# Second attention of a two-layer block: scores by row bands instead of repeated queries and keys, probabilities as the stationary operand

## The reference, cut to what matters

```
x = x + tanh(g_xattn[0]) * attention0(layernorm(x), ctx)      # one head, stage A
x = x + tanh(g_ffn[0])   * experts0(layernorm(x))             # 16 experts of 64, top 4, one shared, stage B
x = x + tanh(g_xattn[1]) * attention1(layernorm(x), ctx)      # 16 heads of 8, stage C
x = x + tanh(g_ffn[1])   * experts1(layernorm(x))             # 8 experts of 128, top 2, stage D

# attention1, for each batch and each of the 16 heads
q = (x @ Wq.T + bq) / sqrt(8);  k = ctx @ Wk.T + bk;  v = ctx @ Wv.T + bv
p = softmax(q @ k.T)            # 128 x 77 for each head
out = concat(p @ v) @ Wo.T + bo
```

## Time and profile before

| | |
|---|---|
| Median of 3 runs | 331.32 us (330.4 to 331.4) |
| The profiled execution's own time | 328.63 us |
| Its span in the trace | 326.7 us, mean granted TensorE clock 0.979 |
| PE, weight loads, DVE, ACT, POOL busy | 289.0, 216.5, 243.6, 163.1, 103.4 us |
| Stages by the trace | A 0 to 39, B 39 to 135.7, C 135.7 to about 244, D to 326.7 us |

### The profile page before, as it was taken

How to read it: one execution, slowest core, us unless ns; L and a number is a source line. 1 busy time by engine, 2 the same in 40 slices (tenths; PEclk the granted TensorE clock), 3 DMA queues, 4 the chain that set the end, 5 groups by cost and what they waited for, 6 DMA issues and landing times.

```text
span 326.7 us, 5592 instructions
## 1 busy us (share of the span) xinstructions
PE 289.0 (88%) x1470; PEld 216.5 (66%) x1470; DVE 243.6 (75%) x714; ACT 163.1 (50%) x435; POOL 103.4 (32%) x160
## 2 busy tenths in 40 slices
PE   6699699989899599589888888988978999999995
PEld 5588476666566376268778778778856667676662
DVE  2887989689579976546697787877968877868572
ACT  1587542432422232676887887889742242332321
POOL 6374200101191510564549539629110010100000
PEclk9999999999979899959999999999999999999999
DMA  6900175586791420000000000000032242151550
GB/s 220 325 25 0 48 225 156 159 231 192 220 246 48 140 98 32 0 2 0 0 4 0 2 1 0 0 0 3 0 108 99 55 155 104 52 178 33 182 174 32
DMA packets 16408, 28.98 MB, mean 89 GB/s; under 512 B 2661, under 2 KB 4659, under 8 KB 16179
## 3 DMA queue, kind: packets, MB, share of 16 engines
q1 hardware_dynamic: 14312, 27.71, 27.6%
q10 hardware_dynamic: 2072, 0.99, 1.2%
HBM read 24.29 MB, written 1.25 MB: 78 GB/s over the span
## 4 chain that ended last, share of the span: by engine, by line
PE 59%; DVE 15%; ACT 9%; DMA 7%; issue 6%; SPq 4%; DVEq 1%; ACTq 0%
PE bank L564 23%; PE Ybank L586 14%; PE bank L757 4%; DMA CR<-comb_rows 3%; ACT PX L1025 3%; DVE cmx L1410 2%; DMA comb_rows<-ct 2%; PE Tb L503 2%; SPq L326 2%; DMA X<-in_x 2%; DVE recT L1426 2%; ACT QS L1013 1%; PE bank L741 1%; PE bank L602 1%; DVE st L1117 1%
## 5 line engine op out<-in xcount | busy, mean ns | idle before, releaser
L908 ACT ACTIVATE sg<-bank 128x512 f32<-128x512 f32 x64 | 38.0, 595 | 73.7 <-PE bank L564 62.0
L1277 DVE TENSOR_TENSOR hb<-sg,CR 128x512 f32<-128x512 f32 x64 | 44.6, 696 | 17.0 <-issue 7.0
L355 POOL TENSOR_TENSOR rstd<-ve,mhalf 128x4 f32<-128x4 f32 x11 | 11.1, 1011 | 131.5 <-DVE ve L1124 131.5
L1270 DVE TENSOR_TENSOR sg<-sg,bank 128x512 f32<-128x512 f32 x64 | 43.5, 680 | 4.5 <-ACT sg L908 2.2
L1410 DVE TENSOR_REDUCE cmx<-bank 128x4 f32<-128x308 f32 x64 | 28.3, 471 | 17.4 <-PE bank L730 17.2
L564 PE MATMUL bank<-xh,WBH 128*128 128x512 f32 x68 | 35.6, 524 | 5.4 <-DVE sg L1270 4.0
L372 POOL TENSOR_TENSOR KS<-kr,CB 128x1232 fp32r<-128x1232 f32 x16 | 36.2, 2268 | 11.3 <-PE bank L730 11.3
L564 PE MATMUL bank<-xh,UPH 128*128 128x512 f32 x64 | 36.2, 565 | 0.0
L586 PE MATMUL Ybank<-hb,W2T 128*128 128x512 f32 x64 | 33.8, 610 | 1.6 <-DVE hb L1277 1.6
L586 PE MATMUL Ybank<-hb,downw 128*128 128x512 f32 x64 | 32.9, 598 | 0.1
L1025 ACT ACTIVATE PX<-bank,cmx 128x77 f32<-128x77 f32 x128 | 29.3, 354 | 0.0
(11 more groups left out here) (184 smaller groups left out, 598.5 us busy)
## 6 DMA issues: line engine op xcount, KB each, us to landing
CR<-comb_rows SPq DMA_DIRECT2D x64, 128.0 KB, 3.2
CR<-comb_rows SPq DMA_DIRECT2D x32, 256.0 KB, 3.4
VX<-in_vs_seed SPq DMA_DIRECT2D x4, 320.0 KB, 5.5
kr<-kh SPq DMA_DIRECT2D x8, 154.0 KB, 3.2
kr<-kl SPq DMA_DIRECT2D x8, 154.0 KB, 3.3
w13raw<-in_w SPq DMA_DIRECT2D x1, 1088.0 KB, 11.4
X<-in_x SPq DMA_DIRECT2D x4, 256.0 KB, 6.5
upraw<-in_up SPq DMA_DIRECT2D x4, 256.0 KB, 4.5
```

The costliest lines, as they stand in the source:

```text
L355: nc.gpsimd.tensor_tensor(rstd[:], ve[:], mhalf[:], ALU.pow).then_inc(rstd_rdy, 1)
L908: A(sg[:, k % 2, :], Gb[k % 2][:], ACT.Silu).then_inc(m.s_done, 1)
L1270: V.tensor_tensor(sg[:, k % 2, :], sg[:, k % 2, :], Ub[k % 2][:], ALU.mult).then_inc(m.t2, 1)
L1277: V.tensor_tensor(hb[:, k % 2, :], sg[:, k % 2, :], CR[:, k % RING, :], ALU.mult).then_inc(m.h_done, 1)
```

## The change

The scores of four heads are made in one band of 32 rows: queries and keys stay where the projections leave them (head h in rows 8h to 8h+7), and each of the four bands has its own bank of PSUM. High and low parts are no longer stacked in rows, but are four matmuls that add up in the bank, so a batch has 16 score matmuls of 32 rows and 308 columns. `QS`, `kr`, `RQ`, `c_repeat` and `place_keys` go away, and POOL expands 616 columns for a batch in place of 1232. The maxima and subtractions take two banks at a time (616 columns), all exponentials have 616 columns and no bias. In the mix the transposed probabilities are stationary and `VX` moves: 9 columns for a head, 8 values and a one, so that the sum of a head comes out beside its result; the rest of the 128 columns are zeros that POOL writes once. The result has queries as rows, needs a reciprocal of 16 columns only, and is transposed (`c_turn`) before the projection; this turn and the projection's result lie in `Tb`. `upraw` lies on the memory of `w13raw` and is loaded first in `later_load`; the `vs_seed` input is gone. The `Fori` loops of stage C on PE, ACT and DVE become Python loops, that is straight code; POOL's stays.

```diff
 def later_load(n):
     if n == 0:
-        sp.wait_ge(k_l, NG)
-    if n < 8:
-        place_keys(2 * n)
-        place_keys(2 * n + 1)
-    elif n < 12:
+        sp.wait_ge(w_split, 10)
+    if n < 4:
...
         sp.dma_start(upraw[:, part], up[:, part]).then_inc(in_up, 16)
-    elif n < 14:
+    elif n < 6:
...
         sp.dma_start(downw[:, part, :], down[:, part, :]).then_inc(in_up, 16)
-    elif n < 18:
...
-        sp.dma_start(VX[:, (n - 14) // 2 * NC * P:((n - 14) // 2 + 1) * NC * P][:, half],
-                     vs_seed[:, half]).then_inc(in_seed, 16)
...
-nc.gpsimd.memset(RQ[:].bitcast(F32), 0.0).then_inc(built, 1)
+nc.gpsimd.memset(Vn[:, :, :, HD:HV], 1.0)
+nc.gpsimd.memset(qq[:, 0].bitcast(F32), 0.0).then_inc(built, 1)
...
 inv_std(NG + 2)
+nc.gpsimd.memset(VX[:], 0.0)
...
-def c_scores(g, t, s, first=False):
+def c_scores(g, t):
     n = GB * g + t
...
+    pe.wait_ge(ks_done, n + 1)
+    if n:
+        pe.wait_ge(c_sub, START + NU * n)
+    for a, b in ((0, 0), (0, 1), (1, 0), (1, 1)):
+        for s in range(NHG):
+            rows = slice(32 * s, 32 * (s + 1))
+            i = mm(bank[s][:, 0:HG * S], qq[rows, g % 2, a, t * P:(t + 1) * P], KT[rows, t % 2, b, :],
+                   start=a + b == 0, stop=a + b == 2)
+    i.then_inc(c_sc, 1)
...
-def c_mix(g, t, u, first):
+def c_mix(g, t, first):
...
+    for c in range(NC):
         w = chunk_rows(c)
-        i = mm(bOut[t % 2][:, u * P:(u + 1) * P], VX[0:w, v:v + P], pt[0:w, c * P:(c + 1) * P],
+        i = mm(bO9[c // CU], pt[0:w, t % 2, c * P:(c + 1) * P], VX[0:w, t % 2, c, :],
                start=c % CU == 0, stop=c % CU == CU - 1)
...
+def c_turn(g, t):
+    n = GB * g + t
+    pe.wait_ge(c_norm, START + n + 1)
+    pe.wait_ge(c_fin, START + n)
+    tr(bOT, On[:].rearrange("p h d -> p (h d)"), I).then_inc(c_ot, 1)
```

More of the change, by code:

```diff
@@ new lines, in c_body @@
+                    n = GB * g + t
+                    before = (g, t - 1) if t else None if first else (g - 1, GB - 1)
+                    if t < GB - 1:
+                        c_scores(g, t + 1)
+                    elif not last:
+                        c_scores(g + 1, 0)
+                    c_transpose(g, t, 0)
+                    if t == 1:
+                        pe.wait_ge(xl_rdy, NG + g + 2)
+                    if t == 2 and not last:
+                        pe.wait_ge(q_l, g + 2)
@@ L1015, in _ @@
[L1015 to L1030 removed]
+                A(qq[:, g % 2, 0, :], Tb[:], ACT.Identity, bias=cols[:, 1:2]).then_inc(q_h, 1)
@@ L1051, in c_body @@
                     n1 = (g, t + 1) if t + 1 < GB else (g + 1, 0)
+                    ahead = t + 1 < GB or not last
+                    c_copy(g, t, 0, first)
                     if t or not first:
[L1053 to L1057 removed]
+                        c_turned(*((g, t - 1) if t else (g - 1, GB - 1)))
+                    if t == GB - 1 and last:
+                        m_route_tanh(mD, 0)
+                    c_copy(g, t, 1, first)
+                    if ahead:
+                        c_exps(*n1, 0)
+                    c_copy(g, t, 2, first)
+                    if t == 0 and not first:
+                        norm_hi(2 * NG + 2 + g, xh[:, slot(g + 1):slot(g + 1) + GT])
                     if t == 1 and not last:
@@ L1060, in c_body @@
                     if t == GB - 1 and last:
-                        m_route_tanh(mD, 0)
                         m_route_copy(mD, 0)
-                    for s in range(NHG):
-                        if t + 1 < GB or not last:
-                            c_exps(*n1, s)
-                        if t == 2 and not last and s != 1:
-                            c_repeat(g + 1, (0, None, 1, 2)[s])
-                    if t == 0:
-                        norm_hi(2 * NG + 2 + g, xh[:, bass.ds(slot(g + 1), GT)])
+                    if ahead:
+                        c_exps(*n1, 1)
+                    if t == 0 and first:
+                        norm_hi(2 * NG + 2 + g, xh[:, slot(g + 1):slot(g + 1) + GT])
             def c_ahead(k):
@@ L1447, in c_body @@
                     before = (g, t - 1) if t else None if first else (g - 1, GB - 1)
-                    before2 = (g, t - 2) if t > 1 else None if first else (g - 1, t + 2)
                     ahead = t + 1 < GB or not last
-                    end = t == GB - 1 and last
+                    if before:
+                        c_normalize(*before)
                     if ahead:
                         c_max(*n1, 0)
-                    if before2:
-                        c_final(*before2)
+                        c_center(*n1, 0)
+                    else:
+                        route_weights(mD, 0)
@@ L1496, in _ @@
-            c_center(0, 0, 3, first=True)
             c_body(0, True, False)
-            with dve.Fori(1, NG - 1) as g:
+            for g in range(1, NG - 1):
                 c_body(g, False, False)
```

407 lines of the change are left out of this document (141 added, 266 removed).

## The result

The changed kernel takes 322.13 us (median of 4 runs, 319.98 to 324.81) against 331.36 us for the kernel before on the same chip (330.4 to 335.08): ratio 0.973, 95% interval 0.967 to 0.979. Ratios and their intervals leave out the runs that lie more than 1.5% above the fastest one of the same kernel; the medians count every run. The profiled execution took 322.10 us with a span of 320.3, 6.4 less than the span before. DVE is relieved a little (237.1 us busy in place of 243.6) and ACT much (129.9 in place of 163.1).

The account below looks back on a forecast made before the run. PE made up 59% of the chain, with PE, ACT and DVE nearly full in C. Terms summed to -8.3 us: 320.3 us profiled, 323.0 us median; range 316 to 329 for the likeliest mechanism, 315 to 339 for all.

Parts of the forecast that it names:

- Bands beside each other, S = 1.0: PE's 16 score matmuls per batch: four bands side by side, four rounds of load and streaming, 1.0 us; best case 0.56.
- rival of loads in a row: Scores of every batch: 16 weight loads pass one way into the array, 1.78 us; 336.1 us in all; chance 0.20.
- that of one after another: Scores of every batch: the 16 matmuls run singly, 2.24 us; 343.8 us in all; chance 0.08.
- The drain: Rival: each change between 32 and 128 rows costs 0.25 us with nothing issued; 331.4 us, no change; chance 0.14.
- T + 2.95: In a turn of C, the mix starts 2.95 us after the batch's first transposes, right behind ACT's third copy.
- Turns 1 to 15, -0.6: Stage C: 14 x 5.2 + 13 x 1.0 = 85.8 us against 86.4, a gain of 0.6.
- Hidden in that idle or behind it: Turns of C: result's turn, projection, norm's transposes, next queries (0.7 us) and DVE's second maximum, subtraction, statistics add no time.
- ACT's and DVE's relief gives room, not time: Stage C: work removed lies off the turn's path; sign: DVE and ACT each busy 4 to 5 us less in four turns.
- Begin, +0.3, at most +1.2: POOL zeroes VX while DVE normalises: 0.3 us lost, at most 1.2, as DVE waits for the ring in any case.
- Fourth and third group, -2.6 and -2.4: Stage B starts: halved key expansions shorten PE's wait, 2.6 us gained; downw loads gone from the ring's way, 2.4 gained.
- First turn, 0: First turn of C, 9.0 us with transposes at 1.2 GHz: PE idles there after the change too, no gain.
- Into C, out of C, end of B: Seams of stages: +1.4 us into C, -2.6 out of C, -1.4 at the end of B.

Follow-up runs that it names:

- copy-first run: Changed kernel with ACT's third copy ahead of the exponential and PE's projection behind the last transposes: 322.62 us, ratio 0.977 to the kernel before.
- early memset: Changed kernel with POOL zeroing VX ahead of its wait for the second group's statistics: 320.65 us, ratio 0.969 to the kernel before.
- bands in series: Changed kernel with the four score matmuls of one band following each other, then the next band: 325.27 us, ratio 0.982 to the kernel before.
- second run of the early memset: Changed kernel with VX zeroed before POOL's wait for statistics, repeated beside the joined versions: 321.0 us, ratio 0.967 to the kernel before.

## Why the prediction held, point by point

The median came at 322.1 us where 323.0 was forecast. That they agree within a us is in part luck: the difference of the profiled executions was -6.4 in place of -8.3, that of the medians -9.2, and several terms were off by 1.5 to 2.1 us in both directions and partly cancelled. The mechanism that was forecast for the scores, the bands beside each other, is the one that ran.

- **Bands beside each other, S = 1.0.** S was 0.77, nearer to the best case. Each band was given 0.11 for a load and 0.14 for streaming in every round; the later bunches of matmuls stand 0.14 us apart, so the loads are hidden after the first. The rival of loads in a row (1.78) and that of one after another (2.24) are refuted by the same 0.77, whatever the order. The drain is real, 0.17 us ahead of the scores and at most 0.13 behind, and too small to decide. One reading behind the loads was off: the 296 ns of the earlier trace rows are a mean of loads from 187 to 338 ns, and loads at half clock took 0.33 us in the kernel after; the 0.111 us of the router's pairs, on which the term rests as well, are not touched by it.
- **The mix as before, 2.26.** It took 2.40 to the first score matmul, 0.17 of it that drain. T + 2.95 was met within 0.01.
- **Turns 1 to 15, -0.6.** It came out +0.9. Thirteen plain turns of 6.13 and the last of 5.27 make 85.0; the other 2.3 us are the turns with the norm's transposes and the next queries (7.03 once, 6.29 to 6.54 otherwise). "Hidden in that idle or behind it" is the step that failed: PE's idle piece of 0.75 us stands ahead of the mix, and it is where these instructions and DVE's waits for them come in.
- **ACT's and DVE's relief gives room, not time.** Shown by the middle of C: ACT 8.5 us less in four turns, the turns 0.5 us shorter. The sign named for it, 4 to 5 us less for each engine, failed for both, ACT's relief being twice that and DVE's only 1.5 us. DVE lost the large reciprocal, but it now subtracts the maximum for all four portions, where ACT's bias did it for two: subtractions take 25.6 us in place of 15.2. That ACT's order sets the turn was argued from the path, and the copy-first run shows it (-0.56 us a turn).
- **Begin, +0.3, at most +1.2.** It cost 2.4, the mis-sized term of the sum. I let DVE's later wait for the ring (1.01 us) cover the memset. But PE doesn't wait for the products behind the ring: it waits for the key instruction that stands right behind the normalising, with no cover, and goes on at 1.2 GHz. Where the clock stayed up behind the same wait the cost was 1.1 us, inside the bound; the half clock, which the term left out, makes the rest. The early memset took back all of it. The Trainium skill ("SBUF — State Buffer", section "SBUF: two separate sides") calls the port pair of DVE and GpSimd an exclusive lock held for the whole instruction; the 2.52 us beside a memset of 2.23 agree, and show that a memset is enough.
- **Fourth and third group, -2.6 and -2.4.** -3.3 and -1.8. The normalising of the fourth group fell from 5.00 to 2.94 us with half of POOL's columns, as forecast; that the expansions cost this much there is shown by the kernel before with them moved, 4.8 us less in that group. At the third group the wait for the ring went as forecast, but POOL's `split_up` now meets the normalising (2.65): a wait that took the place of the one removed, which the sum had not. With that work early the third and fourth group took 1.1 and 1.8 us less again.
- **First turn, 0.** -1.8. It took 7.2 us here, and 6.5 to 9.6 in the profiles of the other versions; PE waits 3.36 to 3.41 us for DVE's subtraction ahead of it in all of them, and the half clock behind lasts longer or shorter; in the 6.5 there is none. That part of the gain is not the change's to claim.
- **Into C, out of C, end of B.** Within 0.4 us each.

What stays open: why the half clock behind the same wait of 3.37 us lasts for different lengths, or stays away, in one kernel, and stage D's +0.5 us, for which no run was made; D takes 79.0 to 79.3 us in the profiles of the changed kernel and its versions.

## What to carry to other kernels

Cut the contraction into row bands when operands would else have to be repeated: here 16 matmuls of 32 rows cost little more than four of 128, and the two orders tried cost the same within 0.03 us. Then look for what the freed engine leaves behind: the turn was set by the order of three copies and two exponentials on ACT, and swapping two of them, with the norm one batch earlier, was worth 4.7 us in turns that the change itself had not shortened. And price every instruction of POOL, a memset too, by which instruction of DVE it will meet and what PE waits for behind that.

## What the runs showed of the hardware that I had not expected

- DVE was held by POOL in large and small instructions that work on SBUF: four normalising instructions of 1.25 us together took 2.52 beside a memset, and four of 1.11 took 2.94 beside expansions of 2.61; a product of 0.69 took 2.76, a 16-column copy 2.21. But not in all: a reciprocal of 128x128 from SBUF to SBUF kept its 0.94 us beside an expansion, and in stage C DVE's maxima and subtractions that read PSUM kept their 0.80.
- Sixteen weight loads of 32 rows fit in 0.58 us, in an order that changes the band each time and (0.62 us) in one that doesn't.
- Fewer moving columns can go with a lower clock: with 72 in place of 128 in the mix, matmuls stood as close as before (0.112 us), and seven of eleven runs had a mean granted clock of 0.955 to 0.976; the one of the seven that was profiled shows it at 0.66 to 0.73 in two stretches of C.
- A wait of PE cost more than itself where half clock followed it, and whether it followed differed between executions: in the second group of B PE waited 1.82 us with the bands in series and 1.81 us in the second run of the early memset; behind the first the clock was 1.00 and the group took 23.0 us, behind the second it was 0.57 from 68 to 76 us and the group took 26.3.
